# Half sums on ScalarE, second copies from SyncE, and four couples added by accumulating DMAs

## The reference

```
e   = stack([tbl_f[ids[:, f]] for f in range(40)], axis=1)      # 512 x 40 x 64
z_p = sum_de e[:, i, d] * W_p[d, e] * e[:, j, e]                # p = (i, j), i < j: 780 of them
h   = concat([z, dense_ctx])                                    # 512 x 796
h   = relu(h @ W_top1 + b_top1)                                 # 512
h   = relu(h @ W_top2 + b_top2)                                 # 256
y   = h @ W_top3                                                # 512 x 1
```

## Time and profile before

| | |
|---|---|
| median of three runs | 354.84 us |
| the profiled execution | 354.51 us |
| its span, first to last instruction | 352.3 us |
| mean granted TensorE clock | 0.976 |
| TensorE busy | 316.6 us, 90% |
| VectorE busy | 250.2 us, 71% |
| GpSimd busy | 233.1 us, 66% |
| ScalarE busy | 219.1 us, 62% |
| ScalarE's sums, L371 | 832 activations, 242 ns each |

### The profile page before, as it was taken

One profiled execution on the slowest core, in us unless ns is written; L12 is line 12 of the kernel. 1 busy time (PEld: TensorE's weight loads), 2 busy tenths in 40 slices (PEclk: granted clock), 3 DMA queues, 4 the chain that ended last, 5 costly groups with the idle time before them and its releaser, 6 DMA issues.

```text
span 352.3 us, 5566 instructions
## 1 busy us (share of the span) xinstructions
PE 316.6 (90%) x1472; PEld 112.1 (32%) x1472; DVE 250.2 (71%) x252; ACT 219.1 (62%) x1696; POOL 233.1 (66%) x194
## 2 busy tenths in 40 slices
PE   0799865999959899999889999999999969999997
PEld 0133423333223333332223333333233323333442
DVE  2375782888728788989759999999999959940000
ACT  1001200467979779779969898897999979600032
POOL 6777777777777767753883899799894953920000
PEclk9999996999989999999989999999999989999999
DMA  6733452333322327632122411423311200000000
GB/s 170 229 105 93 111 146 56 87 97 107 86 58 89 86 79 262 199 95 69 47 75 60 110 45 57 117 64 97 83 41 55 60 0 1 2 0 2 0 0 0
DMA packets 17865, 27.66 MB, mean 79 GB/s; under 512 B 4901, under 2 KB 5029, under 8 KB 17834
## 3 DMA queue, kind: packets, MB, share of 16 engines
q1 hardware_dynamic: 9770, 17.86, 16.9%
q0 software_dynamic: 4608, 4.73, 6.1%
q10 hardware_dynamic: 3456, 4.72, 4.7%
HBM read 22.57 MB, written 0.00 MB: 64 GB/s over the span
## 4 chain that ended last, share of the span: by engine, by line
PE 44%; ACT 25%; POOL 11%; DVE 7%; issue 6%; ACTq 4%; DMA 1%; DVEq 0%
ACT batched L371 24%; PE ps_t L538 18%; PE ps_t L521 8%; PE ps_z L560 7%; POOL rows L319 6%; PE ps_t L586 5%; DVE prod L446 5%; POOL wide_rows L319 5%; ACTq L355 4%; PE ps_t L621 2%; PE ps_e L586 2%; DVE batched L460 2%; PE ps_e L500 1%; ACT E L348 1%; DMA rows<-in_tbl,ids_sb 1%
## 5 line engine op out<-in xcount | busy, mean ns | idle before, releaser
L371 ACT ACTIVATE batched<-batched 128x64 f32<-128x64 f32 x832 | 198.8, 242 | 40.0 <-DVE batched L460 16.6
L446 DVE TENSOR_TENSOR prod<-ps_t,E 128x1024 f32<-128x1024 f32 x148 | 170.9, 1216 | 29.5 <-PE ps_t L538 27.5
L371 ACT ACTIVATION_READ_ACCUMULATOR batched<-batched 128x1 f32 x832 | 156.5, 188 | 0.0
L538 PE MATMUL ps_t<-E,w_sb 64*128 64x512 f32 x592 | 147.4, 621 | 5.5 <-ACT E L348 3.4
L319 POOL DMA_INDIRECT rows<-in_tbl,ids_sb x128 | 121.3, 948 | 38.1 <-issue 37.8
L326 POOL TENSOR_TENSOR prod<-prod 128x1024 f32<-128x1024 f32 x40 | 93.6, 2371 | 32.8 <-DVE prod L446 32.6
L538 PEld LDWEIGHTS ps_t<-E,w_sb 64*128 64x128 f32 x592 | 51.6, 187 | 89.7 <-issue 55.7
L460 DVE TENSOR_TENSOR batched<-ps_t,wide_rows 128x1024 f32<-128x1024 f32 x52 | 60.4, 1218 | 19.4 <-PE ps_t L521 19.2
L521 PE MATMUL ps_t<-w_sb,E 64*128 64x512 f32 x208 | 51.5, 637 | 8.2 <-issue 8.2
L560 PE MATMUL ps_z<-prod,quads 128*32 128x512 f32 x352 | 52.6, 611 | 0.0
L348 ACT ACTIVATE E<-ps_e 128x512 f32<-128x512 f32 x18 | 10.5, 583 | 41.1 <-PE ps_e L489 22.7
(11 more groups left out here) (41 smaller groups left out, 60.8 us busy)
## 6 DMA issues: line engine op xcount, KB each, us to landing
w_sb<-in_w_units SPq DMA_DIRECT2D x50, 256.0 KB, 2.7
E<-E ACTq DMA_DIRECT2D x72, 64.0 KB, 2.1
rows<-in_tbl,ids_sb POOLq DMA_INDIRECT x128
w_sb<-in_w SPq DMA_DIRECT2D x7, 256.0 KB
prod<-in_ids_by_field SPq DMA_DIRECT2D x2, 512.0 KB, 9.1
prod<-in_tbl SPq DMA_DIRECT2D x3, 312.5 KB
w_sb<-in_w SPq DMA_DIRECT2D x1, 512.0 KB
wide_rows<-in_tbl,ids_sb POOLq DMA_INDIRECT x16, 4.3
```

The costliest lines, as they stand in the source:

```text
L371: last = act.activation(products, products, ACT.Copy, accum_out=zt[:, b, at:at + 1])
L446: dve.tensor_tensor(prod[:, n % P_RING, s, :, :], ps_t[:, step % STEPS, :, :], multiplier, ALU.mult).then_inc(product_ready, 1)
L538: last = pe.matmul(ps_t[:, step % STEPS, j, :], w_sb[at:at + DIM, m % W_RING, col:col + P], E[at:at + DIM, slot_of(pairs_of(n)[s][j]), :], ...
```

## The change

ScalarE's sums come in halves (`sum_batched(j, b, i)`: eight sums each), and their place in the order is set by a small budget: each group adds 5, each batched product 10, each copy of a pair takes 2, each half sum costs 4, and half sums are put in while the budget lasts. The second copies of pairs 6 and later are issued by SyncE (`place_fields`), at the pair's place in SyncE's part of the order. Four couples more (7, 8, 11, 13) have their halves added, by DMAs that GpSimd issues with an accumulating operation, one for each group (512 KB from half 1 onto half 0); TensorE waits for a semaphore of the ring slot before it reduces them. The batched products start with k = 13 and 11 in place of 14 and 12, at other unit numbers, which changes which groups there are for those k; pairs 6 and 7 come directly ahead of their first group.

```
-BATCHED = (14, 12, 10, 9, 8, 7, 6, 5, 4, 3, 2, 1, 0)
-BATCHED_AT = (4, 6, 10, 13, 17, 20, 24, 27, 31, 34, 38, 41, 45)
+BATCHED = (13, 11, 10, 9, 8, 7, 6, 5, 4, 3, 2, 1, 0)
+BATCHED_AT = (3, 7, 11, 14, 18, 21, 24, 28, 31, 35, 38, 42, 45)
...
+DMA_COUPLES = (7, 8, 11, 13)
...
 def ahead(u):
-    return 1 if u < 12 else 2
+    return 0 if u in (6, 7) else 1 if u < 12 else 2
...
+PACE = {"group": 5, "batched": 10}
+SUM_COST, COPY_COST = 4, 2
+BY_SCALAR = 6
...
+        def place_fields(eng, u):
+            k = KP - 1 - u
+            if k < 2:
+                return
+            eng.wait_ge(e_copied, place(u) + 1)
+            for f in range(2):
+                for h in range(2):
+                    to, of = (2 * (k % 2) + f) * HALF, f * DIM + h * HALF
+                    eng.dma_start(E4[to:to + HALF, k // 2 - 1, h, :], E[of:of + HALF, slot_of(k), :]).then_inc(
+                        e4_placed[u], 16)
...
             for kind, at in order():
-                if kind == "fields" and at == PARAMS_AT:
-                    load_params()
+                if kind == "fields":
+                    if at == PARAMS_AT:
+                        load_params()
+                    if at >= BY_SCALAR:
+                        place_fields(sp, at)
...
             def add_halves(n):
                 pool.wait_ge(product_ready, FIRST_STEP["group", n] + 2)
+                if n in ADDED_BY_DMA:
+                    pool.dma_start(prod[:, n % P_RING, 0, :, :], prod[:, n % P_RING, 1, :, :],
+                                   accum_op=ALU.add).then_inc(halves_added_by_dma[n % P_RING], 16)
+                    return
...
-            def sum_batched(j, b):
+            def sum_batched(j, b, i):
                 act.wait_ge(product_ready, FIRST_STEP["batched", j] + b + 1)
-                for i in range(2):
-                    for f in range(WIDE):
...
+                for f in range(WIDE):
+                    at = (2 * j + i) * WIDE + f
+                    products = batched[:, (BT * j + b) % B_RING, i, f, :]
+                    last = act.activation(products, products, ACT.Copy, accum_out=zt[:, b, at:at + 1])
                 last.then_inc(batched_summed, 1)
...
                 if kind == "fields" and at >= FIRST:
                     copy_fields(at)
+                    time -= COPY_COST
...
-                elif kind == "group" and left:
-                    sum_batched(*left.pop(0))
+                elif kind in PACE:
+                    if kind == "batched":
+                        left += [(at, b, i) for b in range(BT) for i in range(2)]
+                    time += PACE[kind]
+                    while left and time >= SUM_COST:
+                        sum_batched(*left.pop(0))
+                        time -= SUM_COST
+                    if not left:
+                        time = min(time, 0)
...
-                    if g in ADDED:
-                        pe.wait_ge(halves_added, ADDED.index(g) + 1)
+                    if g in ADDED_BY_POOL:
+                        pe.wait_ge(halves_added, ADDED_BY_POOL.index(g) + 1)
+                    elif g in ADDED_BY_DMA:
+                        pe.wait_ge(halves_added_by_dma[g % P_RING],
+                                   16 * sum(a % P_RING == g % P_RING for a in ADDED_BY_DMA if a <= g))
```

More of the change, by code:

```diff
@@ L75 @@
 DENSE_AT = B_REST
-ADDED_COUPLES = (10, 14, 15, 16, 18, 19, 20, 21, 23, 24, 25, 26, 27, 28, 30, 31, 32, 33, 34, 35)
-ADDED = [n for n in range(NG) if n // 2 in ADDED_COUPLES]
+POOL_COUPLES = (10, 14, 15, 16, 18, 19, 20, 21, 23, 24, 25, 26, 27, 28, 30, 31, 32, 33, 34, 35)
+DMA_COUPLES = (7, 8, 11, 13)
+ADDED_BY_POOL = [n for n in range(NG) if n // 2 in POOL_COUPLES]
+ADDED_BY_DMA = [n for n in range(NG) if n // 2 in DMA_COUPLES]
+ADDED = sorted(ADDED_BY_POOL + ADDED_BY_DMA)
 def arrival(k):
@@ L234, in tower_kernel @@
         halves_added = sem("halves_added")
+        halves_added_by_dma = [sem(f"halves_added_by_dma{i}") for i in range(P_RING)]
         two_reduced = sem("two_reduced")
@@ L339, in copy_fields @@
             def copy_fields(u):
-                k = KP - 1 - u
                 if u < LOOKED_UP:
@@ L347, in copy_fields @@
                     act.wait_ge(e4_placed[u - E_RING], 64)
[L348 to L356, removed]
+                act.activation(E[:, u % E_RING, :], e_bank[u], ACT.Copy).then_inc(e_copied, 1)
+                if u < BY_SCALAR:
+                    place_fields(act, u)
             def copy_rows(u):
@@ L362, in copy_rows @@
                                ACT.Copy).then_inc(rows_copied, 1)
-            def sum_batched(j, b):
+            def sum_batched(j, b, i):
                 act.wait_ge(product_ready, FIRST_STEP["batched", j] + b + 1)
-                for i in range(2):
-                    for f in range(WIDE):
-                        at = (2 * j + i) * WIDE + f
-                        products = batched[:, (BT * j + b) % B_RING, i, f, :]
-                        last = act.activation(products, products, ACT.Copy, accum_out=zt[:, b, at:at + 1])
+                for f in range(WIDE):
+                    at = (2 * j + i) * WIDE + f
+                    products = batched[:, (BT * j + b) % B_RING, i, f, :]
+                    last = act.activation(products, products, ACT.Copy, accum_out=zt[:, b, at:at + 1])
                 last.then_inc(batched_summed, 1)
@@ L375, in _ @@
                 copy_fields(u)
-            left = []
+            left, time = [], 0
             for kind, at in order():
@@ L379, in _ @@
                     copy_fields(at)
+                    time -= COPY_COST
                 elif kind == "rows":
                     copy_rows(at)
-                elif kind == "batched":
-                    left += [(at, b) for b in range(BT)]
-                elif kind == "group" and left:
-                    sum_batched(*left.pop(0))
-            assert len(left) <= (B_REST // (2 * WIDE)) * BT
+                elif kind in PACE:
[7 more added lines that the diff above has]
+                        time = min(time, 0)
+            while left and left[0][0] < P // (2 * WIDE):
+                sum_batched(*left.pop(0))
             act.wait_ge(zt_turned, 1)
             act.activation(z[:, CHUNKS, :], turn_bank[0], ACT.Copy).then_inc(zt_copied, 1)
-            for j, b in left:
-                sum_batched(j, b)
+            for half in left:
+                sum_batched(*half)
             act.wait_ge(zt_turned, 2)
@@ L457, in multiply_batched @@
                     if at >= B_RING:
-                        dve.wait_ge(batched_summed, at - B_RING + 1)
+                        dve.wait_ge(batched_summed, 2 * (at - B_RING + 1))
                     dve.wait_ge(step_done, step + 1)
@@ L597, in _ @@
             pe.wait_ge(e_copied, KP)
-            pe.wait_ge(batched_summed, BT * (P // (2 * WIDE)))
+            pe.wait_ge(batched_summed, 2 * BT * (P // (2 * WIDE)))
             turn_zt(0)
@@ L612, in _ @@
                 sum_h1(m, range(CHUNKS - 1, CHUNKS + 1))
-            pe.wait_ge(batched_summed, BT * NB)
+            pe.wait_ge(batched_summed, 2 * BT * NB)
             turn_zt(1)
```

## The result

The changed kernel takes **343.69 us** (median of four runs, 343.43 to 344.38).

A forecast was written before the change was run, and what follows sets the result against it. TensorE was taken as nearly full, with holes from copies late behind a saturated ScalarE. From 354.51 us, 1.2 by k = 6's batched unit and 4.2 at the last batched unit gave 349.1, as a median 349; range 343 to 356.

The forecast's parts named there:

- a hole at couple 7's reduction: TensorE, reaching couple 7's reduction at 110, waits for accumulations in at 125.7: a new hole of 15 us.
- a small one at couple 8's: A small TensorE hole ahead of couple 8's reduction, whose groups 16, 17 are in at 138.2.
- the early lead: TensorE's gain from the new order, with the 6.95 us hole gone; all lost by groups 24, 25, 3.5 us behind.
- the late holes: TensorE's holes of late copies ahead of 177.74 (2.53 us) and 286.95 (3.31 us) go.
- three stretches: TensorE up to groups 24, 25: +3.5 us; then to k = 6's batched unit: -4.7; then to the end: -4.2.
- a pair is in 10.5 us after its first issue starts: Accumulating DMAs issued by GpSimd: first landing 6.8 us, second 3.7 more, so a pair in 10.5 us.
- rival 1: Quick accumulations, a pair in 5 us: groups 24, 25 start 5.5 us earlier, 343.6 us; chance 0.2.
- The walk to k = 6: TensorE from groups 24, 25 to k = 6's batched unit: 41.0 us in place of 45.7, starting at 180.8.
- The start: TensorE from 77 to couple 7's reduction: 6.5 units, four reductions and three transposes, arriving at 110.
- what goes: ScalarE's second-copy issues for 12 pairs, 12 x 2.44 = 29.3 us out of a full queue.
- SyncE: at no cost: SyncE's 48 more issues of about 0.33 to 0.6 us cost nothing; without cover up to 5 us at each even pair.
- Couples 11 and 13: Their accumulations do not hold TensorE: groups 22, 23 are in at 155.5 and wanted near 159.

The follow-up runs named there:

- lead of 8: The changed kernel with GATHER_LEAD = 8 in place of 14, so accumulating DMAs are issued ahead of more gathers: 333.23 us, ratio 0.9383.
- lead of 10 and no accumulating DMAs: The changed kernel with GATHER_LEAD = 10 in place of 14 and DMA_COUPLES = (): 335.64 us, ratio 0.9425.
- one part alone: Two runs of the kernel before: second copies from pair 6 issued by SyncE, 339.61 us; couples 7, 8, 11, 13 added by DMA, 361.27 us.

## Why the prediction was right, and 5 us too high

**The mechanism was right, some sizes were not.** The forecast said a hole at couple 7's reduction set by GpSimd's place in the queue, a small one at couple 8's, the early lead lost, the late holes gone; the trace has each. The forecast's own time misses by 4.7 us of the profiled execution. It lies in two of the three stretches, 2.4 in the first and 2.35 in the second; the third came out as forecast, to 0.1 us partly by luck, as 0.4 of it lies outside the span.

**The couples by DMA: "a pair is in 10.5 us after its first issue starts".** This is the term of the first stretch. The line L353 in two windows that hold one issue each, couple 7's first and second:

```profile
L353 POOL DMA_DIRECT2D prod<-prod x1: 1022/1022/1022, 115.3 to 115.3; - x1
...
DMA to landing us min/median/max: 5.6/5.6/5.6
```

```profile
L353 POOL DMA_DIRECT2D prod<-prod x1: 1317/1317/1317, 116.0 to 116.0; - x1
...
DMA to landing us min/median/max: 7.7/7.7/7.7
```

A landing is counted from the issue's own start, so couple 7 is in at 123.7, some 8.3 us after its first issue starts, and so is couple 8 (from 127.4; 128.0 + 7.7). The first landing of a pair was taken at 6.8 us; it is 5.6 for couple 7, 4.7 for couple 8, and 5.8 and 5.2 for couples 11 and 13. The second was put 3.7 us behind the first by the time that its data takes; it lands 2.7 and 3.5 us behind it for couples 7 and 8. So the two do queue, a little less than forecast, and most of the 2.2 us is a first landing put too long. An issue was taken at 1.25 us; two take 1.95, since their rows overlap, so 0.97 each. Couple 8's reduction starts at 135.83 in place of 138.2. The time equals that of rival 1 (343.6), but not by its mechanism: a pair in 5 us was not seen.

The Trainium skill, "DMA: Bandwidth & Descriptors" (Anatomy of one DMA — SWDGE path), gave an estimate of 3.2 us for one accumulation; the fastest of the eight took 4.7, so for this kind of transfer the trace doesn't agree.

**The walk to k = 6: 41.0 us, measured 38.69.** Of the 45.74 of before, the prediction took off the hole of 177.74, the slowed matmuls behind it and half a reduction for each of couples 11 and 13. It left out the reduction behind that hole, which the trace of before has slowed too:

```profile
180.19 1.94 PE L560 MATMUL ps_z<-prod,quads 128*32 128x512 f32 x8
```

Without the hole it takes 1.06 (0.9). The groups directly behind batched products, 4.4 us before, take 3.9 and 4.0 (0.8). The last 0.6 is spread over several units and has no single cause. Together 2.3.

**The start was later than forecast, at no cost.** TensorE reached couple 7's reduction at 113.8, not at 110: the two holes at 47.93 and 70.22 were not foreseen (2.3 us, as pair 8's transposes start at 79.33 in place of 77), and the walk from there takes 34.4 us in place of 33. The second hole is a copy behind two half sums that wait for VectorE; ScalarE's timeline:

```profile
65.72 0.26 ACT L393 ACTIVATE batched<-batched 128x64 f32<-128x64 f32 x1 [6.36 <-DVE batched L489]
...
69.55 0.57 ACT L377 ACTIVATE E<-ps_e 128x512 f32<-128x512 f32 x1
```

The transposes of pair 7 end near 67.5 and the copy starts 2 us later, about the 1.92 of one half sum that the prediction named as the most. But pairs 6 and 7 have no group between transposes and use, so here it isn't hidden: 2.64 us, and 1.7 more for a unit at the lower clock. GpSimd's wait swallows it in the changed kernel. In the version with a lead of 8 the hole is there too (70.24), but TensorE's hole isn't in the chain there: up to 144 us that is GpSimd's gathers, additions and accumulating DMAs, so it costs nothing either. With a lead of 10 and no accumulating DMAs the chain does run through it (2.50 us ahead of 69.98).

**ScalarE: right in what goes, wrong in what takes it away.** The prediction let the late holes go because of issues, halves and pacing together. The runs with one part alone and with whole sums show that the issues do it. What the prediction did not say is that this part by itself is worth more than the whole change. The Trainium skill's "DMA: Bandwidth & Descriptors" (Issuing engines are not separate DMA queues) says that issuing from another engine only saves the sequencer's time, usually small beside the transfer. It is exactly that time which is saved here, 12 sets of 2.44 us; but on a queue that is full and that others wait for, it is 4.4% of the kernel.

**SyncE: at no cost, as taken.** Its 48 issues have a median of 591 ns, and no engine waited for a second copy in the changed kernel. **Couples 11 and 13** are in before they are wanted, as forecast.

## What to carry to other kernels

Ask of each part of a change which queue it leaves and which it enters, and where in program order: here 0.6 us issues taken from the full queue gave 4.4%, and half-megabyte additions put behind a queue of 10 us gathers took part of it back (0.9% by the version without the two early ones). An instruction that others wait for belongs ahead of prefetches in a queue that runs in program order; that alone was worth 2 to 3% here, without any change to the work. Price what stands behind a hole too: where the granted clock had fallen, a unit of 16 matmuls right after one took 5.1 to 5.4 us in place of 3.7 (6.67 in the version with a lead of 10 and no accumulating DMAs).

## What the runs showed of the hardware

Accumulating DMAs can disturb more than their own queue. In the stretch where they run the DMA engines' share rises from 0.40 to 0.72 (0.44 in the version without them); the windows of before and of after (columns as in the earlier trace rows):

```profile
110.00:176.00 66.00, 63.45 (x342) 21.62 (x340) 55.47 (x50) 55.93 (x454) 45.38 (x39) 1.00 0.40 118
```

```profile
110.00:176.00 66.00, 54.95 (x270) 18.88 (x266) 49.98 (x44) 49.31 (x398) 55.59 (x50) 0.92 0.72 175
...
120.00:130.00 10.00, 6.19 (x22) 2.23 (x24) 2.75 (x3) 2.88 (x25) 8.22 (x9) 0.58 0.54 105
```

Plain issues of other engines can slow down meanwhile. In the kernel before with the couples by DMA, ScalarE's 16 issues in the four sets named there take 0.98 us on average, 1.9 at most, the 32 others from pair 6 on 0.62. With a lead of 8, SyncE's sets at 114.19 and 140.49 us, with accumulations under way, take 5.45 and 4.55 us; the ten others take 2.41 to 3.42. But in the changed kernel SyncE's set at 152.48 us takes 2.42 with couple 11's second accumulation still under way, and a single issue took 2.36 us where nothing accumulates (SyncE, with the issues moved alone). What makes an issue slower, the runs don't show. GpSimd's own addition isn't slower: its row at 128.64 lasts 3.12 us, but starts before the issues' row ends (127.44 + 1.95), and it ends 2.37 us behind that, as long as an addition takes. And the clock: over the 10 us from 120 on, the end of couple 7's hole and the batched unit behind it, the granted clock is 0.58 on average, nearer the lower of its two levels (1.2 and 2.4 GHz), and that unit takes 5.08 us in place of 3.70.
